# The first stage's residual sum: on VectorE, or in PSUM by TensorE with ScalarE copying it out

## What is computed

```python
x = x + _L0_attn_ref(_layernorm(x), Wk, bk, Wv, bv, Wr, br, Wo, bo, ...)   # the first stage
x = x + _L0_xattn_ref(_layernorm(x), ctx_512, ctx_512)                     # the second stage
...
# inside _L0_attn_ref (RWKV):
xk = x_prev + (x - x_prev) * tmk        # and xv, xr alike
k  = xk @ Wk.T + bk                     # and v, r alike
wkv = scan over the 128 tokens of (k, v), with a running maximum pp and sums aa, bb
out = (sigmoid(r) * wkv) @ Wo.T + bo
```

## Time and profile before

| what | us |
|---|---|
| median of 3 runs | 1420.72 (1419.54 to 1421.12) |
| the profiled execution's own time | 1405.85 |
| its span (first to last instruction) | 1404.0 |
| the first stage in it | 0 to 137.5 |

### The profile page before, as it was taken

The page is one execution under the profiler, slowest core; times in us unless marked ns, Lnnn a source line. Parts: engine busy times, 40 slices in busy tenths (PEclk is TensorE's granted clock), DMA queues, the critical chain, the costliest instruction groups (busy, mean ns, idle before and its releaser), DMA issues. The chain is left out here.

```text
span 1404.0 us, 24766 instructions
## 1 busy us (share of the span) xinstructions
PE 1216.4 (87%) x7679; PEld 943.2 (67%) x7726; DVE 960.2 (68%) x1863; ACT 760.1 (54%) x1757; POOL 603.5 (43%) x737
## 2 busy tenths in 40 slices
PE   6895899989989983499989999999977888869998
PEld 5673444467879873377777777777754555648887
DVE  5999899836755358877877778777854666633443
ACT  5433577753555453566666666666643555533332
POOL 2000556352164553766676666666644333320000
PEclk9997999969999996699999999999997999989999
DMA  9001000010035313200000000000000000000000
GB/s 330 2 1 55 14 16 17 9 61 1 16 106 150 93 55 154 109 1 1 1 0 0 0 0 0 0 0 0 1 1 6 3 3 3 3 1 1 16 15 31
DMA packets 27422, 44.74 MB, mean 32 GB/s; under 512 B 5648, under 2 KB 22160, under 8 KB 25936
## 3 DMA queue, kind: packets, MB, share of 16 engines
q1 hardware_dynamic: 23888, 34.31, 7.1%
q0 software_dynamic: 3456, 9.44, 2.6%
HBM read 32.21 MB, written 9.44 MB: 30 GB/s over the span
## 5 line engine op out<-in xcount | busy, mean ns | idle before, releaser
L2312 ACT ACTIVATE wi_weights<-wi_psum,wi_bias,wi_scale 128x128 f32<-128x128 f32 x256 | 113.7, 454 | 120.1 <-DVE wi_bias L2432 120.1
L2087 POOL TENSOR_TENSOR wi_straight<-wi_straight,wi_crossed 128x512 f32<-128x512 f32 x80 | 103.0, 1287 | 10.9 <-DVE wi_crossed L2418 10.8
L975 DVE TENSOR_REDUCE gq_least<-gq_psum 128x4 f32<-128x512 f32 x128 | 84.6, 686 | 13.8 <-PE gq_psum L858 12.1
L2075 POOL TENSOR_TENSOR wi_scratch<-wi_sums,wi_eps 128x4 f32<-128x4 f32 x80 | 33.7, 421 | 131.0 <-DVE wi_sums L2391 129.6
L2076 POOL TENSOR_TENSOR wi_scale<-wi_scratch,minus_half 128x4 f32<-128x4 f32 x80 | 84.6, 1057 | 6.3
L2202 PE MATMUL wi_psum<-wi_k_t,wi_q_t 128*128 128x128 f32 x512 | 68.3, 277 | 20.7 <-ACT wi_q_t L2303 19.5
L937 ACT ACTIVATE gq_weights_t<-gq_psum 128x512 f32<-128x512 f32 x128 | 67.7, 601 | 23.4 <-PE gq_psum L878 23.2
L2153 PEld LDWEIGHTS wi_psum<-const,wi_straight 128*128 128x128 f32 x320 | 39.1, 142 | 55.9 <-issue 37.4
L2852 DVE TENSOR_REDUCE cr_top<-cr_psum 128x4 f32<-128x512 f32 x64 | 43.7, 682 | 46.4 <-PE cr_psum L2667 46.4
L2423 DVE TENSOR_REDUCE wi_top<-wi_psum 128x4 f32<-128x512 f32 x64 | 43.9, 686 | 45.9 <-PE wi_psum L2202 45.9
L2211 PE MATMUL wi_psum<-wi_weights_t,wi_values 128*128 128x512 f32 x128 | 68.1, 613 | 2.8 <-DVE wi_weights_t L2439 1.3
(11 more groups left out here) (415 smaller groups left out, 3818.8 us busy)
## 6 DMA issues: line engine op xcount, KB each, us to landing
slot_y<-ex_s_out SPq DMA_DIRECT2D x20, 256.0 KB, 2.5
x<-in_x_dram SPq DMA_DIRECT2D x4, 512.0 KB, 7.9
gate<-in_gate_dram SPq DMA_DIRECT2D x2, 1024.0 KB, 6.4
up<-in_up_dram SPq DMA_DIRECT2D x2, 1024.0 KB, 8.4
down<-in_down_dram SPq DMA_DIRECT2D x2, 1024.0 KB, 10.5
egu<-in_egu_dram SPq DMA_DIRECT2D x1, 2048.0 KB, 15.9
gq_keys_diagonal<-gq_key_parts SPq DMA_DIRECT2D x64, 32.0 KB, 1.9
wo<-in_wo_dram SPq DMA_DIRECT2D x1, 2048.0 KB, 8.8
```

Source lines behind the costliest of these rows:

```text
L975: dve.tensor_reduce(least[:, n // 2 % 2, n % 2, j, :], ps[:, j % 2, :].rearrange("p (v t) -> p v t", t=P), AX.X, ALU.min).then_inc(topped, 1)
L2087: added_up = pool.tensor_tensor(straight[:, at], straight[:, at], crossed[:, at], ALU.add)
L2312: act.activation(weights[:, g % 2, j, :], ps[:, SC + g % 2, j * P:j * P + P], ACT.Exp, bias=bias[:, g % 2, j:j + 1], scale=scale[:, g, j:j ...
```

## The change

Three things are changed, all in the first stage.

- PE: after the bias of group g it multiplies the group's x, 128 x 512 for each of the two banks, with the unit matrix and accumulates that onto the bias (new L374). The bank then ends up as the new x itself. The matrix is fp32, as x is.
- ACT: a new helper `keep_sum(g)` waits for the bank's `out_ready` and copies the bank, 128 x 512, over x (new L460), two instructions per group. It stands in ACT's program in rounds 2 and 3 for groups 0 and 1, right after `pad_h` and ahead of `take` of k; for groups 2 and 3 it stands after the last round, ahead of the clear of `gq_keys_diagonal`.
- DVE: `add` becomes `measure`, the four statistics alone, which wait for ACT's copies (`added`). Group 0 is measured in round 2 and group 1 in round 3, one round later than before; groups 2 and 3 after the last divide, as before.

```diff
             def bias(g):
...
                     pe.matmul(ps[:, out_bank(g) + i, :].rearrange("p (j d) -> p j d", d=D), net.ones[0:1, 0:P], bo,
                               start=True, stop=False)
+                pe.wait_ge(net.in_x[g], 16)
+                for i in range(2):
+                    b = GB * g + 2 * i
+                    pe.matmul(ps[:, out_bank(g) + i, :], ident, net.x[:, b:b + 2, :].rearrange("p b d -> p (b d)"),
+                              start=False, stop=False)
...
+            def keep_sum(g):
+
+                for i in range(2):
+                    b = GB * g + 2 * i
+                    act.wait_ge(out_ready, 2 * g + i + 1)
+                    act.activation(net.x[:, b:b + 2, :].rearrange("p b d -> p (b d)"), ps[:, out_bank(g) + i, :],
+                                   ACT.Copy).then_inc(added, 2)
...
             def one(g):
                 pad_h(g)
+                if g >= 2:
+                    keep_sum(g - 2)
                 take(g, 0)
...
             for g in range(1, NG):
                 one(g)
+            for g in (NG - 2, NG - 1):
+                keep_sum(g)
             act.wait_ge(projected, 3 * KC * NG)
             zero = net.ones[:, 0:1].broadcast_to([P, 4 * KV_HEADS * P])
             act.activation(net.kbd_all[:], zero, ACT.Copy, scale=0.0).then_inc(net.zeroed, 1)
...
-            def add(g):
+            def measure(g):
                 for i in range(2):
-                    dve.wait_ge(out_ready, 2 * g + i + 1)
+                    dve.wait_ge(added, GB * g + 2 * i + 2)
                     for j in (2 * i, 2 * i + 1):
-                        b = GB * g + j
-                        dve.tensor_tensor(net.x[:, b, :], net.x[:, b, :],
-                                          ps[:, out_bank(g) + i, (j % 2) * D:(j % 2) * D + D],
-                                          ALU.add).then_inc(added, 1)
-                    for j in (2 * i, 2 * i + 1):
-                        dve.wait_ge(added, GB * g + j + 1)
                         own.did(dve.bn_stats(net.stats[:, GB * g + j, :], net.x[:, GB * g + j, :]))
...
                 accumulate(g)
-                if not first and not last:
-                    add(g - 1)
-                    if g == 1:
+                if g >= 2:
+                    measure(g - 2)
+                    if g == 2:
                         measure_first()
                 own.again()
...
             divide(NG - 1)
-            add(NG - 2)
-            add(NG - 1)
+            measure(NG - 2)
+            measure(NG - 1)
```

## The result

The changed kernel takes 1425.14 us (median of 15 runs, 1423.61 to 1429.02); the kernel before, run beside it, 1419.54 (15 runs, 1414.26 to 1424.17). The ratio is 1.0049, with a 95% interval of 1.0036 to 1.0062: **slower by about 7.0 us, 5.1 to 8.8**. The direction and the place of the loss are as predicted; the time lies 3.4 us under the range of 1428.5 to 1437. A difference given with an interval is the ratio times the median of before; the plain difference of two medians lies up to 1.9 us from it (5.6 us here).

The account below looks back on a forecast made before the run. The first stage was taken as a chain on DVE, its end moving everything behind the barrier. Waits and products 3.2 plus uncovered clear and issues 8.7 made 11.9 us; 1420.7 + 11.9 = 1432.6, range 1428.5 to 1437.

Parts of the forecast that it names:

- The barrier and what it waits for: First stage's end: clear and nine SP issues follow the last copy, lose their cover and cost 8.7 us.
- The place of the copies: Rounds two and three: copies ahead of k leave DVE idle 4.3 and 3.6 us before the scans.
- The added products: PE, behind each bias: two fp32 products of 512 columns, four records, take 1.72 us per group.
- the clock over output 1: PE, round three: the granted clock falls over group 1's output as before, 5.06 us for 16 records.
- rival (a): Round three's clock: no fall, path 1.7 us shorter, 1430.9, chance 0.20; fall before the new products, 1434.3, chance 0.08.
- The second step: After the barrier: both traces run parallel, 11.9 us apart, with 1 us each way allowed for the clock.
- the base: Starting time of the sum: the kernel before's median, 14.9 above the profiled execution's own time, 1420.7.
- (b): First stage: ACT's waits cost DVE nothing, banks coming earlier; barrier at 142.1, +4.3, total 1425; chance 0.02.
- (c): Barrier: SP's issues don't hold it; it opens with the clear at 143.8, +6, total 1426.7; chance 0.03.
- (d): First stage's end: DVE's relief decides, clear and issues ending before it; 5.2 us earlier, 1415.5; chance 0.01.
- (e): Second stage: the later keys' transfer holds up key DMAs and a tile; +3, total 1435.6; chance 0.06.

Follow-up runs that it names:

- e2: The changed kernel with ACT's clear of the key tile put back ahead of the last two copies: 1418.79 against 1418.55, ratio 1.0004.
- e11: The kernel before, unchanged, run and profiled a third time: 1415.19 against 1418.03, ratio 0.9993.
- e8: The kernel before with two added 512-column products of one row of zeros behind each bias: 1422.03 against 1419.33, ratio 1.0029.
- e4: The kernel before with three unused long reciprocals on DVE at the first stage's end, a bare delay: 1429.55 against 1418.55, ratio 1.008.
- e7: The kernel before with one short unused reciprocal on DVE at the first stage's end: 1422.61 against 1419.33, ratio 1.0024.
- e10: The kernel before with two long unused reciprocals on DVE at the first stage's end: 1421.67 against 1418.03, ratio 1.0038.
- e3: The kernel before with ACT's clear made to wait for the last output bank: 1424.92 against 1418.55, ratio 1.0038.
- e5: e2 with ACT's copies in rounds 2 and 3 put behind k and the next normalising: 1421.12 against 1419.33, ratio 1.0017.

## Why the prediction was right in its mechanism and wrong in its size

**The barrier and what it waits for: right.** Clear and nine issues were put at 3.70 + 5.89 + 0.3 us behind the last copy. Measured: 137.59 to 147.59, 10.0 us, of which DVE's last statistics cover the first 0.9. The 8.7 us that it was to cost are 8.5 between the starts of after and e2, 8.8 by DVE's idle time.

**The place of the copies: right, smaller.** I had 4.3 and 3.6 us of idle time ahead of the two scans; they are 4.04 and 1.64. The scan of group 2 was to be 1.2 us later and is 0.5, because PE's bias came at 66.67 rather than 67.27 and the copies take 0.60, not 0.65. The early bias is luck of the trace: the clock had come back to full at about 63.9 instead of 64.7, and e11, the kernel before, has that too, with its bias at 66.72. (The Trainium skill, "ScalarE: Activation LUTs", section "What ACT_TABLE_LOAD costs", gives 186 ns + 0.833 ns per element for an ACTIVATE with immediate scale and bias, 0.61 us for 512; the copies out of PSUM agree.)

**The added products: right.** 1.82 us from their first record to the output, in both rounds, for the 1.72 that I took. The figure of 216 ns a record, which the prediction quoted from "TensorE: Matmul & The Clock Gate" of the Trainium skill (section "Back-to-back issue gap"), would have made it 0.86; the trace speaks against it for these fp32 products.

**The step that failed first: the clock over output 1.** The forecast let it fall as before, 5.06 us for the 16 records; it stayed full, and the next products start 100.74 - 97.48 = 3.26 us after it. That is rival (a), to which I gave 0.20: 1.7 us less, measured 1.8. The hint was in the rows that I named myself: the fall had come behind a bias that uses one row of the array, and the change puts full-array work exactly there. All five traces with that work keep the clock, and e8, with one-row products in the same place, loses it. With this and the 0.4 us by which the second round was early, the second stage starts at 147.6 and not at 149.7: +9.8 and not +11.9. By (a) alone I had 1430.9.

**The second step: "from there on the two traces should run parallel".** They don't, in either direction. The second stage takes 154.8 us in after and 153.1 in before, as its clock is low for longer; I had allowed 1 us, it is 1.7. The windows of its first 16 us, of before and of after:

```profile
137.00:153.00 16.00, 9.43 (x36) 5.44 (x39) 10.88 (x32) 3.98 (x7) 10.38 (x11) 0.79 0.07 16
```
```profile
147.00:163.00 16.00, 10.12 (x27) 6.21 (x27) 9.72 (x28) 3.26 (x6) 10.39 (x11) 0.50 0.38 117
```

It isn't the change's own doing alone, nor that of the late start: e11, the kernel before, has 154.7 too, with a clock of 0.58 over the same stretch of the stage, and e4, which starts at 147.8 as after does, has 153.1 with 0.70. Then the router gives 3 to 6 us, and the third and fourth stages spread by up to 10. Bare delays show that on the mean a step at the barrier arrives whole: 20.2 us in three comparisons for 18.6 inserted. But a single comparison carries this spread: by the medians 5.6 us in the first one, 8.7 and 8.4 in the two repeats, for a step of 9.8; by the ratios 7.0, 9.4 and 9.4.

**The sum.** Of the 7.5 us between 1432.6 and 1425.14, 2.1 are the smaller step at the barrier, shown. 1.2 are the base: 1420.72 was a median of three runs, that of fifteen is 1419.54 (1418.0 to 1419.3 in the other comparisons). The other 4.2 are 9.8 - 5.6, the part of the step that the first comparison doesn't show; the repeats show all but 1.1 to 1.4 of it. That this is the spread of the later stages and not something the changed kernel gives back is argued from e4, e7 and e10, not shown; 1 to 3 us stay open. The medians of the repeats, 1427.98 and 1426.39, lie under 1428.5 too. The prediction's range had no term for the spread of the base, though a profile that lay 15 us under the median of its own kernel was a sign of it.

**The rivals.** (b), the waits cost nothing, fell with the 4.04 us in front of the scan. (c), SP's issues don't hold the barrier, fell with 9.15 us of idle DVE that end just behind the ninth issue, and with e3. (b) had a slip in its sum as well: the adds, statistics and aggregates gone from round one are 74.83 - 71.76 = 3.1 us, not 2.8. (d) fell: even with the clear early (e2), taking sixteen adds off DVE wins nothing, since DVE then waits for ACT or PE. (e), the later keys' transfer: the key products begin at 152.86, 5.3 us after ACT's first work of the stage, as in the earlier trace rows, so it cost nothing there. The small key DMAs land in a median of 2.4 us instead of 1.9, but e10 and e11, where that transfer is over long before, have as long a second stage (154.5 and 154.7).

**Is there a better version?** No run beat the kernel before. e2 and e5 are equal to it within their intervals (0.9987 to 1.0021 and 0.9999 to 1.0035). PE has no gap from the bias of one round to the end of that round's projections and turn (73.94 to 86.47 in e5), so products added there push back what DVE takes up next. That this keeps any such version from being faster than before is argued from e5, not shown. No run has the copies without the products, or the full-array products without the copies.

## What to carry to other kernels

When work is moved onto an engine with idle time, look at what stands behind the new place in that engine's order: ACT was idle for 14 us here, and the moved copies still delayed k by 7 us and more, and the clear with its nine DMA issues by 23.5 us (114.06 in e2, 137.59). A step that nobody waits for, such as a clear with the DMAs that it releases, belongs ahead of everything that waits for the last result, or the next barrier pays for it. And before a sum is trusted to 0.3%, run the unchanged kernel again: two of its traces differed by 10 us in stages that the change never touched.

## What the runs showed of the hardware that was not expected

**A busy PE can lose its clock.** In before and e8 PE has no gap in the third round from 92 us until its clock falls, and yet the granted clock goes from 2.4 to 1.2 GHz behind products that use one row of the array: 95.4 to 98.8 us in before, 70.9 to 74.3 and 98.2 to 105.0 in e8, which has twice as many of them. With full-array products in the same place it stays at 1.0, and once, in e10, it stays there behind the bias alone. The Trainium skill ("TensorE: Matmul & The Clock Gate", section "What's actually happening") says that the gate follows how busy the PE has been recently; by their records PE is busy without a gap in all these stretches, so busy time alone doesn't sort them.

**The same kernel has several lengths of one stretch.** The router took 16.9, 16.9 and 14.0 us in three traces of before, 11.1, 11.1 and 11.0 in three of after, by how much of it was at half clock: the mean granted clock over it is 0.50, 0.50 and 0.61 there, and 0.80, 0.79 and 0.80 here. Where the low stretches of the clock fall differs by run and by kernel; why is open.

**Waits that nothing shows.** In the third stage ACT and DVE wait for something "remote", ACT alone at line `ex_gated` for 4 to 14 us in all, in every trace but the first of before. What it is stays open. Of the 13 us by which the times of the unchanged kernel spread (1411 to 1424) it may be a good part.
